# A transformer decoder layer on one core: new orders of work on four engines in the attention steps

## What is computed

```python
x = x + attn(layernorm(x), Wv, bv, Wo, bo)      # q = k = v = layernorm(x) @ Wv.T + bv
x = x + xattn(layernorm(x), ctx, ctx)           # no projections: q is layernorm(x), k = v = ctx
x = x + ffn(layernorm(x))                       # shared expert and top 1 of 7 experts, SwiGLU, I = 352
```

## Time and profile before

| | us |
|---|---|
| timed runs, median of 3 (lowest to highest) | 415.33 (414.82 to 415.68) |
| profiled execution, span from the first to the last instruction | 427.0 |
| PE busy in the span | 404.4 |
| DVE, ACT, POOL busy | 305.1, 298.5, 284.8 |
| PE's granted clock, mean | 0.992 of full speed |

### The profile page before, as it was taken

How to read it: one execution, slowest core, us unless ns; L and a number is a source line. 1 busy time by engine, 2 the same in 40 slices (tenths; PEclk the granted TensorE clock), 3 DMA queues, 4 the chain that set the end, 5 groups by cost and what they waited for, 6 DMA issues and landing times.

```text
span 427.0 us, 16199 instructions
## 1 busy us (share of the span) xinstructions
PE 404.4 (95%) x5545; PEld 312.9 (73%) x5546; DVE 305.1 (71%) x791; ACT 298.5 (70%) x684; POOL 284.8 (67%) x476
## 2 busy tenths in 40 slices
PE   7989999999998999999999898969999999999997
PEld 4646666666665666666665667959988999999996
DVE  7868999999998998999999787713333444444444
ACT  7659999999998999999998685302213466666651
POOL 8757788878887888888888423665664463444442
PEclk9999999999999999999999999996999999999999
DMA  6254566767676667765444300021113255430001
GB/s 104 43 85 64 87 103 108 109 110 121 120 124 117 114 123 126 143 101 84 60 63 43 35 2 2 27 81 58 69 69 90 67 133 139 131 104 27 27 32 52
DMA packets 176324, 35.22 MB, mean 82 GB/s; under 512 B 145587, under 2 KB 174646, under 8 KB 176256
## 3 DMA queue, kind: packets, MB, share of 16 engines
q1 hardware_dynamic: 71296, 21.43, 23.1%
q10 hardware_dynamic: 102144, 6.81, 15.2%
q0 software_dynamic: 2816, 6.10, 4.1%
HBM read 20.86 MB, written 15.67 MB: 86 GB/s over the span
## 4 chain that ended last, share of the span: by engine, by line
PE 68%; DMA 10%; issue 6%; DVE 6%; ACT 3%; SPq 2%; POOL 2%; another core or an unknown queue 2%; DVEq 0%; ACTq 0%; POOLq 0%
PE psum L867 15%; PE psum L659 12%; PE psum L668 12%; PE psum L973 8%; PE psum L680 7%; DMA orow<-attention_out 3%; DMA attention_out<-on_s 3%; PE psum L690 3%; SPq L198 2%; DMA ring<-sorted_rows 2%; PE psum L763 2%; PE psum L802 2%; PE psum L758 1%; PE psum L809 1%
## 5 line engine op out<-in xcount | busy, mean ns | idle before, releaser
L1583 DVE TENSOR_TENSOR gT<-gT,psum 128x384 f32<-128x384 f32 x66 | 36.5, 553 | 77.5 <-PE psum L867 34.4
L1263 ACT ACTIVATE gT<-psum 128x384 f32<-128x384 f32 x70 | 33.6, 488 | 58.4 <-PE psum L867 36.9
L620 POOL DMA_INDIRECT out<-yrow,token x38 | 37.1, 975 | 41.2 <-DVE yrow L1718 22.0
L973 PE MATMUL psum<-wdn_sb,gT 128*128 (+1 forms) x420 | 60.2, 280 | 4.0 <-DVE rows_all L1597 2.2
L479 POOL TENSOR_TENSOR k_s<-pT,hmask_sb 128x1024 f32<-128x1024 f32 x32 | 61.0, 1906 | 0.9 <-ACT pT L1137 0.8
L973 PEld LDWEIGHTS psum<-wdn_sb,gT 128*128 128x128 f32 x420 | 53.3, 195 | 5.7 <-issue 2.7
L867 PE MATMUL psum<-fhT,wtile 128*128 128x128 f32 x456 | 57.2, 275 | 0.3 <-ACT wtile L1292 0.3
L867 PE MATMUL psum<-hT_all,wup_sb 128*128 128x128 f32 x384 | 50.9, 283 | 5.0 <-issue 3.8
L867 PEld LDWEIGHTS psum<-fhT,wtile 128*128 128x128 f32 x456 | 53.9, 192 | 0.5 <-ACT wtile L1292 0.5
L867 PEld LDWEIGHTS psum<-hT_all,wup_sb 128*128 128x128 f32 x384 | 47.7, 198 | 6.0 <-issue 4.8
L1065 ACT ACTIVATE pr_x<-pr_x,rs 128x512 f32<-128x512 f32 x60 | 43.0, 722 | 8.2 <-DVE pr_x L1368 7.0
(11 more groups left out here) (193 smaller groups left out, 872.0 us busy)
## 6 DMA issues: line engine op xcount, KB each, us to landing
sorted_rows<-nowhere_row SPq DMA_DIRECT2D x38, 130.0 KB, 3.6
ring<-sorted_rows SPq DMA_DIRECT2D x30, 130.0 KB
wup_sb<-in_wup SPq DMA_DIRECT2D x14, 176.0 KB, 3.0
orow<-attention_out SPq DMA_DIRECT2D x31, 64.0 KB
ring<-in_ctxv ACTq DMA_DIRECT2D x60, 32.0 KB, 3.7
cross_keys<-in_ctxk ACTq DMA_DIRECT2D x14, 128.0 KB, 3.7
ring<-cross_keys SPq DMA_DIRECT2D x112, 16.0 KB
rows_all<-in_x ACTq DMA_DIRECT2D x10, 128.0 KB, 3.9
```

The costliest lines, as they stand in the source:

```text
L620: pool.indirect_dma_start(out=out, out_offset=bass.IndirectOffsetOnAxis(ap=token[p][:, 0:1], axis=0), in_=yrow[p][:, :], in_offset=None, b ...
L973: last = nc.tensor.matmul(ps_y[p], gT[place_of(n) if isinstance(n, int) and n < FIRST else p][:, c, :], wdn_sb[:, expert, c, :], start=(c ...
```

## The change

The same instructions are issued, in another order. On PE: the output's transpose moves from the end of a step to the next step, between the two halves of the self turning; the projection moves behind it, between the two halves of the self weighing; the transpose of the normalised input stands between the two halves of the cross turning; both halves of the cross weighing precede the cross scores. On DVE, from step 5 on: the self output is inverted and normalised ahead of the self subtraction, the moments of x and of the input come behind it. On ACT: the copies of the turned output, of the values and of the turned input come later. On POOL: the masked keys come first from step 4 on, and centring comes ahead of the bias and the cross addition. In the tail PE turns the last looped output between two self halves. The cross maxima and subtraction remain single instructions over two banks.

```diff
@@ -450,9 +450,21 @@
...
+            def keys_masked(u):
...
             def body(t, u, live):
                 i = t % 2
                 pool.wait_ge(sem("mv_set"), 2)
+                late = t >= LAG["q"]
+                if live("proj") and late:
+                    keys_masked(u["proj"])
...
@@ -464,23 +476,25 @@
...
                 if live("norm"):
                     normed("p", t, u["norm"], xn["p"][:], "p_xT")
-                if live("proj"):
...
+                if live("proj") and not late:
+                    keys_masked(u["proj"])
                 if live("st_x"):
                     normed("x", t, u["st_x"], h_all[:, u["st_x"], :], None)
+                if live("q"):
...
+                    nc.gpsimd.tensor_scalar(xn["s"][:], x_all[:, u["q"], :], mv[i][:, 0, 0:1], None,
+                                            ALU.subtract).then_inc(sem("s_xn"), 1)
...
+                    nc.gpsimd.tensor_scalar(ve[:, 0:1], mv[i][:, 0, 1:2], EPS, float(DK), ALU.add, ALU.mult).then_inc(sem("s_ve"), 1)
                 if live("xb"):
...
@@ -490,17 +504,6 @@
...
                     nc.gpsimd.tensor_tensor(x_all[:, u["on_x"], :], x_all[:, u["on_x"], :],
                                             on["x"][:].rearrange("p a c d -> p (a c d)"), ALU.add).then_inc(sem("x_x"), 1)
...
-                    nc.gpsimd.tensor_scalar(xn["s"][:], x_all[:, u["q"], :], mv[i][:, 0, 0:1], None,
-                                            ALU.subtract).then_inc(sem("s_xn"), 1)
...
-                    nc.gpsimd.tensor_scalar(ve[:, 0:1], mv[i][:, 0, 1:2], EPS, float(DK), ALU.add, ALU.mult).then_inc(sem("s_ve"), 1)
                 if live("q"):
...
@@ -765,20 +768,18 @@
             def body(t, u, live):
                 if live("soft_s"):
                     turn("s", u["soft_s"], 0)
+                if live("q"):
+                    turn_output(u["q"])
+                if live("soft_s"):
                     turn("s", u["soft_s"], 1)
-                if live("q"):
-                    project(u["q"])
                 if live("on_x"):
                     turn_back("x", u["on_x"])
-                if live("xT"):
-                    pe.wait_ge(sem("p_xn"), at(u["xT"]))
-                    if u["xT"] >= 1:
-                        pe.wait_ge(sem("p_v"), u["xT"])
-                        pe.wait_ge(sem("p_pT"), u["xT"])
-                    nc.tensor.transpose(ps_xT, xn["p"][:], id_sb[:]).then_inc(sem("p_xT"), 1)
                 if live("soft_s"):
                     pe.wait_ge(sem("p_v"), at(u["soft_s"]))
                     weigh("s", u["soft_s"], 0, v_s[u["soft_s"] % 2][:])
+                if live("q"):
+                    project(u["q"])
+                if live("soft_s"):
                     weigh("s", u["soft_s"], 1, v_s[u["soft_s"] % 2][:])
                 if t == 1:
                     keep_clock(3, bank[3])
@@ -787,6 +788,13 @@
                     scores("s", u["S_s"], pT, k_s)
                 if live("pv_x"):
                     turn("x", u["pv_x"], 0)
+                if live("xT"):
+                    pe.wait_ge(sem("p_xn"), at(u["xT"]))
+                    if u["xT"] >= 1:
+                        pe.wait_ge(sem("p_v"), u["xT"])
+                        pe.wait_ge(sem("p_pT"), u["xT"])
+                    nc.tensor.transpose(ps_xT, xn["p"][:], id_sb[:]).then_inc(sem("p_xT"), 1)
+                if live("pv_x"):
                     turn("x", u["pv_x"], 1)
                 if live("soft_s"):
                     turn_back("s", u["soft_s"])
@@ -794,6 +802,8 @@
                     keep_clock(2, bank[3])
                 if live("q"):
                     query(u["q"])
+                if live("pv_x"):
+                    cross_weighed(u["pv_x"], (0,))
                 if live("xT"):
                     pe.wait_ge(sem("p_xnT"), at(u["xT"]))
                     for b in range(NB):
@@ -815,13 +825,9 @@
                 if t < 3:
                     keep_clock(1 if t == 0 else 4, bank[3])
                 if live("pv_x"):
-                    cross_weighed(u["pv_x"], (0,))
+                    cross_weighed(u["pv_x"], (1,))
                 if live("q"):
                     cross_scores(u["q"])
-                if live("pv_x"):
-                    cross_weighed(u["pv_x"], (1,))
-                if live("out"):
-                    turn_output(u["out"])
 
             phase_a(body, last=LAST_FULL)
 
@@ -881,6 +887,7 @@
                 up(n, place_of(n), wup_sb[:, E, :], hT_all[:, n, :])
 
             turn("s", U - 1, 0)
+            turn_output(U - 3)
             turn("s", U - 1, 1)
             pe.wait_ge(sem("p_v"), U)
             pe.wait_ge(sem("p_pT"), U)
@@ -1127,6 +1134,17 @@
...
+            def values_out(u):
+
+                if u >= 2:
+                    act.wait_ge(sem("s_pv"), G * (u - 1))
+                act.wait_ge(sem("p_pv"), at(u))
+                for h2 in range(2):
+                    rows = slice(S * h2, S * (h2 + 1))
+                    last = nc.scalar.copy(v_s[u % 2][rows, :].rearrange("p (a b e) -> p b a e", a=HP, b=NB)[:, :, :, DK * h2:DK * (h2 + 1)],
+                                          ps_v[rows, :].rearrange("p (b a d) -> p b a d", a=HP, b=NB))
+                last.then_inc(sem("p_v"), 1)
+
             def body(t, u, live):
                 if live("proj"):
                     act.wait_ge(sem("p_p"), at(u["proj"]))
@@ -1135,14 +1153,8 @@
...
-                if live("proj"):
...
+                if live("proj") and t < LAG["q"]:
+                    values_out(u["proj"])
                 if live("soft_s"):
                     exp("s", u["soft_s"], 0)
                     exp("s", u["soft_s"], 1)
@@ -1150,18 +1162,15 @@
                     second_store(u["out"])
                 if live("on_x"):
                     evicted("x", u["on_x"])
+                if live("soft_s"):
+                    turned("s", u["soft_s"], 0)
                 if live("q"):
                     output(u["q"])
                 if live("soft_s"):
-                    turned("s", u["soft_s"], 0)
                     turned("s", u["soft_s"], 1)
+                if live("proj") and t >= LAG["q"]:
+                    values_out(u["proj"])
                 bulk_of_step(t)
-                if live("xT"):
...
-                    nc.scalar.copy(xnT[:], ps_xT).then_inc(sem("p_xnT"), 1)
                 if live("pv_x"):
                     exp("x", u["pv_x"], 0)
...
@@ -1172,6 +1181,13 @@
                     evicted("s", u["soft_s"])
                 if live("pv_x"):
                     turned("x", u["pv_x"], 0)
+                if live("xT"):
+                    act.wait_ge(sem("p_xT"), at(u["xT"]))
+                    if u["xT"] >= 1:
+                        act.wait_ge(sem("p_p"), u["xT"])
+                        act.wait_ge(sem("p_pv"), u["xT"])
+                    nc.scalar.copy(xnT[:], ps_xT).then_inc(sem("p_xnT"), 1)
+                if live("pv_x"):
                     turned("x", u["pv_x"], 1)
                 if live("out"):
                     cross_values(u["out"], 1)
@@ -1394,36 +1410,40 @@
 
             X_LOADS = {0: ("l_x0", 16), 2: ("l_x1", 16), 4: ("l_x4", 16), **{n: (f"l_x{n}", 16 if n == RING else 32) for n in range(RING, U, 4)}}
 
+            def first_moments(u):
+
+                if u in X_LOADS:
+                    dve.wait_ge(sem(X_LOADS[u][0]), X_LOADS[u][1])
+                moments("p", u)
+
             def body(t, u, live):
-                if live("norm"):
-                    if u["norm"] in X_LOADS:
-                        dve.wait_ge(sem(X_LOADS[u["norm"]][0]), X_LOADS[u["norm"]][1])
-                    moments("p", u["norm"])
+                ahead = t < LAG["pv_x"]
+                if live("norm") and ahead:
+                    first_moments(u["norm"])
+                    mean_variance("p", t, u["norm"])
                 if live("st_x"):
                     normalise("x", u["st_x"])
-                if live("norm"):
-                    mean_variance("p", t, u["norm"])
                 if live("pv_x"):
                     mean_variance("s", u["pv_x"] + LAG["q"], u["pv_x"])
                 if live("soft_s"):
                     maxima("s", u["soft_s"])
+                if live("out"):
+                    invert("s", u["out"])
+                    normalise("s", u["out"])
+                if live("soft_s"):
+                    soften("s", u["soft_s"], 0)
+                    soften("s", u["soft_s"], 1)
                 if live("st_x"):
                     dve.wait_ge(sem("x_x"), at(u["st_x"]))
                     moments("x", u["st_x"])
-                if live("out"):
-                    invert("s", u["out"])
-                if live("out") and t < LAG["q"]:
-                    normalise("s", u["out"])
+                if live("norm") and not ahead:
+                    first_moments(u["norm"])
                 if live("st_x"):
                     mean_variance("x", t, u["st_x"])
-                if live("soft_s"):
```

(7 more changed lines are left out.)

38 lines of the change are left out of this document (11 added, 27 removed).

## The result

The changed kernel takes **423.89 us** (median of 4 runs, 422.88 to 424.15) against 415.5 (median of 4, 414.82 to 415.93) for the kernel before on the same chip: ratio **1.0203, 95% interval 1.0184 to 1.0221**, 8.4 us slower. Forecast were 421.8 us, 417.5 to 426.5, with 0.84 on slower.

A forecast was written before the change was run, and what follows sets the result against it. The prediction took the cross-scores loop through PE, DVE and ACT as the limit. Its terms 6.8 + 0 + 0 - 1.2 + 0.9 + 0 gave +6.5, so 421.8 us from 415.33, range 417.5 to 426.5.

The forecast's parts named there:

- Part 1: PE: both cross weighing halves ahead of the cross scores lengthen the loop by 0.25 per step, +6.8 us (to +10.0).
- The loop that I drew: Steady step: cross scores, DVE maxima and subtraction, ACT exponentials, PE back to the next scores; 7.09 us, claimed as limit.
- Part 2: ACT and PE: copying the normalised input between the two turned cross halves costs nothing, with 0.1 us to spare.
- Part 3: DVE: inversion and normalisation ahead of the subtraction make a second loop of 7.38, tying with the first at 7.34.
- Part 4: Attention output turned later and normalised earlier: shorter waits for its reload, -1.2 us, ends -0.5 and -2.2.
- Part 5: POOL: cross output's addition behind the centring delays DVE's moments at the last full step's end, +0.9 us, ends 0 and 1.3.
- Part 6: First steps: step 4's earlier normalisation (+0.3) set off against a reload wait saved; 0, ends -0.4 and +0.4.
- the interval is long but DVE has no wait for the scores: Sign named in advance that would show the forecast reading wrong, seen between cross scores in steady steps; no size.
- PE is the limit (faster): Rival: PE's work sets the steady interval, so filling PE's waits gains time; 409.1 us, chance 0.10.
- DVE is the limit already: Rival: DVE's work sets the 7.09 us step in any order, so no change; 415.0 us, chance 0.06.
- The new wait takes over at 7.7: Rival: DVE waits for the self output's turning back every step, the second loop reaching 7.7; 431.2 us, chance 0.08.

The follow-up runs named there:

- PE's order alone: Kernel before, with only the first cross weighing half moved ahead of the value projection and the second directly ahead of the cross scores; ratio 1.0089.
- input's turn alone: Kernel before, with only the normalised input's transpose and copy moved between the two cross halves; ratio 1.0048.
- inversion back: Changed kernel with DVE's inversion and normalisation of the self output again behind the self subtraction; ratio 1.0155.
- PE's half back: Changed kernel with the second half of the cross weighing again behind the cross scores; ratio 1.0211.
- both back: Changed kernel with the self output's inversion and normalisation behind the self subtraction and the second cross weighing half behind the cross scores; ratio 1.0204.
- and moments back: Changed kernel with self inversion, normalisation and second cross weighing half put back, plus the first stream's moments and aggregation ahead of the self maxima; ratio 1.0126.

## Why the prediction was right, and where it was not

**Part 1, PE's halves: right in mechanism, 0.19 instead of 0.25.** Shown by the kernel with that order alone. The loop that I drew had "no idle time left over in it", but its rows left out ACT's query copy, which ended last ahead of the scores; and a half ahead of the value projection shortens the projection's own distance. 27 x 0.19 = 5.1 instead of 6.8. The medians of the steps show the loop in three pieces: from the scores to the cross maxima, from these to the second exponential, from this to the next scores. Beside them stands the distance from the end of ACT's query copy to the scores. The first two kernels below "before" are the kernel before with one part of the change, the last four the changed kernel with parts taken back:

| kernel | scores to maxima | maxima to exponential | exponential to scores | copy to scores | interval |
|---|---|---|---|---|---|
| before | 1.22 | 3.32 | 2.53 | 0.05 | 7.08 |
| PE's order alone | 1.23 | 3.32 | 2.72 | 0.25 | 7.27 |
| input's turn alone | 1.23 | 3.33 | 2.61 | 0.06 | 7.16 |
| changed | 1.26 | 3.31 | 2.74 | 0.27 | 7.31 |
| inversion back | 1.23 | 3.33 | 2.74 | 0.26 | 7.29 |
| PE's half back | 1.47 | 3.32 | 2.52 | 0.05 | 7.31 |
| both back | 1.43 | 3.32 | 2.56 | 0.05 | 7.30 |
| and moments back | 1.29 | 3.31 | 2.62 | 0.05 | 7.21 |

**Part 2, the copies "cost nothing": met, but not by my working.** I looked at what the weighing halves wait for, and not at the other users of ACT and PE between the second exponential and the scores: the query copy comes later, and so do the turning back and the value projection. Alone that costs 0.08 per step. In the changed kernel the two prices don't add up to 0.27: PE's path is the longer one there, the scores come 0.27 behind the query copy, and 2.74 instead of the 2.72 of PE's order alone is all that the move could have added. It is nearly free only because part 1 is paid.

**Part 3, the second loop and the tie: right as far as it went.** In the step shown both loops are 7.37 (140.27 to 147.64). In the median step PE's would be 1.22 + 3.31 + 2.74 = 7.27, and DVE, arriving late, makes it 7.31; my 7.34 was 0.03 above. Undoing one of the two gives 7.29 or 7.31. But there was a third of the same length, self scores to self maxima to moments to cross maxima, and with both undone the interval stays at 7.30. By my own test, "the interval is long but DVE has no wait for the scores", the reading that PE's path is *the* limit failed: it is one of at least three. From 7.08 to the 7.21 with all three undone, 0.09 stand between the second exponential and the scores, which follow ACT's query copy by 0.05, and 0.07 between the scores and the cross maxima, for which DVE has no wait; no run separates them.

**Part 4, the reload: sign right, size open.** Above 27 times their median interval the steps of the kernel before have 2.5 us in one profile and 1.8 in the other, those after 1.65. So 0.2 to 0.9 was gained, not 1.2. And PE's order alone, with the output turned where it was, leaves 0.35: a longer step is enough for that gain, and no run shows one from turning the output later. Waits for the reload are gone from steady steps, but five steps of the changed kernel take 7.5 to 7.7. In one of them (7.62) the exponentials come late. In three (7.65 to 7.68) the cross maxima begin 1.60 behind the scores, and DVE stood idle for 0.26 to 0.29 ahead of them or of the aggregation before them, for nothing that the profile shows. Why isn't known.

**Part 5, POOL and the end: right.** +0.95 against +0.9, given back by putting only the last full step's order back. The rows that answer to the earlier trace rows, where the idle was 0.53:
```profile
239.99 0.41 POOL L505 TENSOR_TENSOR rows_all<-rows_all,on_x 128x128 f32<-128x128 f32 x1
...
240.44 0.29 DVE L1356 BATCH_NORM_STATS2 st_x<-rows_all 128x6 f32<-128x128 f32 x1 [1.70 <-POOL rows_all L505]
```
**Part 6, first steps "0": wrong, +3.39.** I priced only step 4. In steps 0 to 3 the cross stream isn't there, so a piece moved "between the cross halves" is moved behind the self scores with nothing to cover it: 1.2 of it is shown by the kernel with the turn alone. Another 0.57 is there at the self scores of step 1 (10.09 against 9.52) and isn't the change's: two kernels with the same order up to there have 9.51 and 9.52. In step 4 the inversion and normalisation ahead of the self subtraction cost 0.37, near the +0.3 that I had set off against the reload. They stand there in that step too; of what the section on the change puts "from step 5 on", only the input's moments wait until then. From the self scores of step 3 to the turned halves of step 4 it takes 4.25 here and 4.26 with PE's half back, but 3.89 in all three kernels with the inversion behind the subtraction. From there to the cross scores it takes 6.72 with the clock's fall (below) and 6.02 in those three, without it: 0.70. Some 0.5 is left, in all of these kernels, and no run gives it to a part.

The rivals. *PE is the limit (faster)*: filling PE's waits gained nothing; PE's busy time went from 404.4 to 406.6 and the kernel became slower. Weighed against the rule of the Trainium skill ("Perfetto Trace Analysis", "Optimization Strategies") that the prediction named, the measurement decides against it here: its second half, to work on what blocks the critical path, is the part that holds. *DVE is the limit already*: excluded by PE's order alone, which cost 0.19 per step. The 0.21 that the prediction sets against the Trainium skill, "VectorE: DVE Perf Modes", section "The DRAIN you can't avoid", doesn't contradict it: that section also says that an operation which isn't held starts earlier. *The new wait takes over at 7.7*: the wait is there (21 steps), the price is 7.3.

## What to carry to other kernels

Where a kernel has been balanced, several loops have nearly the same length. Undoing one part then shows nothing, and doing one part alone on the kernel before can show its price, as it did for two of three here; the third, DVE's order, needed the others and showed only that. Make both before calling a part harmless or guilty. For each instruction that is moved into a loop, list all users of that engine between the loop's two ends (here ACT's query copy, which ends last ahead of the scores, and the score banks that wait for the last copy), and cost the first steps separately: what covers a moved piece in the steady state may not exist yet.
